# Last stage of a graph network kernel: second exponential and row turn exchanged on ScalarE, first slot sum and scan projection on TensorE

## What is computed

```python
# graph attention of the last layer
e = leaky_relu(s_src[src] + s_tgt[tgt], 0.2)
exp_e = exp(e - max(e)); denom = segment_sum(exp_e, tgt)
agg = segment_sum(proj[src] * (exp_e / (denom[tgt] + 1e-16))[:, :, None], tgt)
# scan (mamba) over x[perm]
xc, z = split(xs @ in_proj_w.T)
xc = silu(conv4(xc) + conv_b)
dbc = xc @ x_proj_w.T                          # 16 for dt, 16 for B, 16 for C
dt = softplus(dbc[:, :16] @ dt_proj_w.T + dt_proj_b)
dA = exp(dt[:, :, None] * A); dBx = (dt * xc)[:, :, None] * B[:, None, :]
h = dA_t * h + dBx_t;  y_t = h @ C_t           # for t in order, 16 states per channel
y = (y + xc * D_param) * silu(z);  return y @ out_proj_w.T
```

## Time and profile before

| | |
|---|---|
| median of 3 runs | 8897.0 us (8894.1 to 8900.4) |
| profiled execution | 8896.2 us, its span 8894.4 us |
| last stage | 6,424 us to 8,420 us of the span |
| PE busy in the span | 4623.8 us (52%) |
| DVE busy | 4836.3 us (54%) |
| ACT busy | 1231.8 us (14%) |
| POOL busy | 5163.8 us (58%) |

### The profile page before, as it was taken

How to read it: one execution, slowest core, us unless ns; L and a number is a source line. 1 busy time by engine, 2 the same in 40 slices (tenths; PEclk the granted TensorE clock), 3 DMA queues, 4 the chain that set the end, 5 groups by cost and what they waited for, 6 DMA issues and landing times. The chain is left out here.

```text
span 8894.4 us, 95573 instructions
## 1 busy us (share of the span) xinstructions
PE 4623.8 (52%) x18992; PEld 3629.7 (41%) x18993; DVE 4836.3 (54%) x11590; ACT 1231.8 (14%) x2744; POOL 5163.8 (58%) x4985
## 2 busy tenths in 40 slices
PE   4008244544457777656666555545454555554354
PEld 3002133333356666644444344433344444444333
DVE  9462388888822222245455344444466666666644
ACT  1002011111101111100000000001122222222111
POOL 0021366766667777677777677777655556555400
PEclk6557677677778888877777677777677777667676
DMA  0201256555423333233333233333222332222200
GB/s 8 75 16 52 59 143 170 161 159 162 130 80 94 92 90 94 69 84 99 92 95 95 63 83 96 89 92 92 75 85 83 91 91 83 86 86 80 71 6 9
DMA packets 485777, 772.81 MB, mean 87 GB/s; under 512 B 296031, under 2 KB 316310, under 8 KB 481979
## 3 DMA queue, kind: packets, MB, share of 16 engines
q0 software_dynamic: 265504, 666.90, 27.1%
q10 hardware_dynamic: 19838, 70.21, 2.1%
q1 hardware_dynamic: 200345, 34.81, 2.1%
HBM read 822.37 MB, written 46.03 MB: 98 GB/s over the span
## 5 line engine op out<-in xcount | busy, mean ns | idle before, releaser
L794 POOL DMA_INDIRECT gat_rows<-scratch_gat,gat_index x1856 | 1857.4, 1001 | 576.3 <-issue 540.0
L1071 PE MATMUL gat_ps<-gat_work,k_ident 128*128 128x256 f32 x3712 | 1214.3, 500 | 933.2 <-DVE gat_work L865 817.6
L1645 POOL DMA_INDIRECT m_rows<-scratch_gat,m_index x928 | 1097.1, 1182 | 861.0 <-DVE m_work L1934 581.5
L1071 PEld LDWEIGHTS gat_ps<-gat_work,k_ident 128*128 128x128 f32 x3712 | 941.3, 260 | 1213.2 <-issue 900.4
L794 POOL DMA_INDIRECT conv_rows<-scratch_kv,conv_index x928 | 931.9, 1004 | 410.7 <-issue 267.6
L1071 PE MATMUL conv_ps<-conv_work,k_ident 128*128 128x256 f32 x1856 | 668.4, 538 | 851.2 <-DVE conv_work L865 779.5
L1211 POOL DMA_INDIRECT rel_rows<-scratch_x,rel_index x928 | 926.7, 999 | 286.5 <-issue 273.8
L1071 PEld LDWEIGHTS conv_ps<-conv_work,k_ident 128*128 128x128 f32 x1856 | 511.8, 283 | 1008.2 <-issue 821.2
L1698 PE MATMUL m_ps<-m_work,k_ident 128*128 128x256 f32 x1664 | 524.2, 487 | 359.2 <-DVE m_work L1934 359.2
L1443 PE MATMUL rel_ps<-rel_factor,rel_rows 128*128 128x128 f32 x3712 | 581.6, 330 | 214.6 <-DMA rel_rows<-scratch_x,rel_index 214.6
L1443 PEld LDWEIGHTS rel_ps<-rel_factor,rel_rows 128*128 128x128 f32 x3712 | 563.2, 244 | 226.8 <-DMA rel_rows<-scratch_x,rel_index 154.5
(11 more groups left out here) (453 smaller groups left out, 7840.3 us busy)
## 6 DMA issues: line engine op xcount, KB each, us to landing
m_bc<-scratch_bc ACTq DMA_DIRECT2D x25, 2048.0 KB, 8.6
gat_rows<-scratch_gat,gat_index POOLq DMA_INDIRECT x1856
conv_rows<-scratch_kv,conv_index POOLq DMA_INDIRECT x928
rel_rows<-scratch_x,rel_index POOLq DMA_INDIRECT x928
m_rows<-scratch_gat,m_index POOLq DMA_INDIRECT x928
scratch_runs<-e_runs_sb SPq DMA_DIRECT2D x1, 12890.6 KB
scratch_kv<-p_row ACTq DMA_DIRECT2D x25, 256.0 KB
gat_index<-scratch_slots SPq DMA_DIRECT2D x232, 4.0 KB, 1.8
```

Source lines behind the costliest of these rows:

```text
L794: pool.indirect_dma_start(out=rows[b][:, s, :], out_offset=None, in_=table, in_offset=bass.IndirectOffsetOnAxis(ap=index[b][:, s:s + 1], a ...
L1071: ins = pe.matmul(ps_sum[min(b, 1)], ident, work[b][:, s, :], start=s == 0, stop=s == S - 1)
L1645: pool.indirect_dma_start(out=rows[b][:, s, :], out_offset=None, in_=dr["gat3"], in_offset=bass.IndirectOffsetOnAxis(ap=index[b][:, s:s + ...
```

## The change

```diff
@@ TensorE, tile(t, has_front, ahead) @@
                 w = Visit(pe, kp, t)
-                sum_slots(w, 0, 0)
                 if has_front:
                     front(t + 1)
+                sum_slots(w, 0, 0)
                 sum_states(t)
@@ ScalarE, tile(t, has_front, ahead) @@
                     spread_bc(t + 1)
+                exp(w, 0, 1)
                 if ahead:
                     turn(t + 2)
-                exp(w, 0, 1)
-                if ahead:
                     gates(t + 2)
                 store(t)
```

## The result

The changed kernel takes 8664.4 us (median of 4 runs, 8663.9 to 8673.8) against 8896.0 us (median of 4 runs, the three shown above and one of 8895.1): 0.974 of the time before, 95% interval 0.973 to 0.975. That is 231.6 us less. The prediction was 8659 us, within 8620 to 8735. The profiled execution of the changed kernel is the longest of its four runs, 8673.8 us; it starts tile 0 of the last stage at 6429.3 us, 5.1 us later than the profile before (6424.2), though nothing was changed ahead of it.

A forecast was written before the change was run, and what follows sets the result against it. VectorE's chain was taken to set the last stage's period, in five-chunk tiles together with GpSimd's gathers. 136 us (ScalarE's exchange) + 102 (TensorE's) = 238 us off 8896.2 is 8658, given as 8659 us; range 8620 to 8735.

The forecast's parts named there:

- The wait of the second chunk: VectorE's wait for ScalarE's exponential of the second gather, in tiles 0 to 22: 6.41 us falls to 0.27 us.
- The new wait for the scan input: VectorE waits some 0.5 us per tile for TensorE's scan input; the convolution still starts 5.6 us earlier.
- The second slot sum: TensorE's sum of the second gather takes 3.62 us instead of 5.40, so it doesn't delay the output product.
- the rival of the lower clock: More TensorE groups fall to 1.2 GHz and the second slot sum takes 6.54 us: 8727 us; chance 0.15.
- The third exponential: ScalarE's exponential of the third chunk, behind the store of the scan's output: its 2.62 us wait stays.
- TensorE gains clock: Rival: the denser last stage is granted 2.4 GHz sooner: 8624 us at most, 8641 us for half; chance 0.10.
- The projection: At a tile's head, the copy's wait falls from 4.57 to 0.7 us in 24 tiles; the projection takes 0.64 us.
- The moved slot sum costs nothing: TensorE's first slot sum, now after the projection, ends at least 2.8 us before the next state sums: no cost.
- Five-chunk tiles: Tiles 3 to 12: earlier release of the second gather's buffer shortens the next tile's gather wait, 0.7 us each, 7 us.
- part 1: ScalarE's exponential of the second chunk ahead of the turn of t + 2: 136 us in sum.
- the slower rival: GpSimd's gather issues, stretched under VectorE's scans, become the bound; slower only above 22.5 us per tile: 9000 us; chance 0.03.
- The signs of being wrong: Scan-input wait over 1.5 us, late output product, decays or first slot sum waited for, gather waits above 79.5 us.

The follow-up runs named there:

- the repeat: The changed kernel run once more, unchanged, as base for later kernels: 8665.4 us, 0.974 of the kernel before; its profiled run took 8662.5 us.
- a padded kernel: Three memsets of 1.85 us on GpSimd ahead of its wait for buffer 1, twice per tile, added to the changed kernel: 8810.3 us.
- the same eight extra matmuls: Eight matmuls that nobody reads, at the head of each tile ahead of the projection, added to the changed kernel: 8664.4 us.

## Why the prediction was right

- **The wait of the second chunk**: 150.6 us, forecast to fall to 0.27 us in each of 23 tiles. It fell to 6.2 us. Tile 23 had shown it before the change.
- **The new wait for the scan input**: forecast 0.5 us per tile, 11.5 in all; measured 21.4 in 22 tiles. The step that sized it took the pace of one tile's second sums of states (5.72 us) for all, though they already ranged from 5.2 to 6.8 us; they take 6.06 us on average in this profile, 6.45 in tile 11. It varies between runs: in the repeat's profile they take 5.87 us and the wait is 15.0 us in 20 tiles. That the convolution starts some 5.6 us earlier whatever the pace was right: E + 14.28 before, E + 9.35 here, with the sums 0.73 us longer.
- **The second slot sum**: I took 3.62 us by the neighbourhood of the earlier trace rows against the 5.40 of the earlier trace rows. It is 3.62 us in all 23 tiles, and the output product waits for y and not the other way. This is the choice between the forecast and the rival of the lower clock, and it was right for this group, with ScalarE's exchange alone as well.
- **The third exponential**: forecast to stay as it is. Its wait fell from 71.8 to 61.4 us over 23 tiles: 12 of them had waited 3.6 us behind an output product that took 2.07 us, and it takes 1.13 us now. The rival "TensorE gains clock" had named this. These 10 us are as much as the scan input cost too much.
- **The projection**: forecast 0.7 us of wait left in each of 24 tiles, with 0.9 as the upper bound; measured 1.07. The step that failed is "the projection takes 0.64 us": that row was read directly behind a slot sum, at a granted clock of 1.00, and the exchange puts a pause of 4 us or more there, behind which it is 0.50. With 1.08 us the term is 92.7 us instead of 101.6. The bound of 0.9 was too tight.
- **The moved slot sum costs nothing**: nearly. Its result is waited for by nobody, but TensorE's exchange alone brought 83 us where the projection's wait fell by 93; the difference appears as longer waits for exponentials. In the changed kernel these don't grow; there the wait for the scan input is the longer one, 21.4 and 15.0 us in the two profiles against 9.8 without the moved slot sum, where the second sums of states take 5.60 us on average.
- **Five-chunk tiles**: forecast 0.7 us more than the others in each, so 6.3 us of part 1. They gained 10.0 us each, the four-chunk tiles 9.7; of this the projection's wait gave 3.4 and 4.2, which leaves 6.7 and 5.5 us for part 1. The mechanism (gathers hold the next tile's first logits) was right: the release moved by 6.7 us on average, from E + 10.8 to E + 4.2, and the distance from it to the next tile's first logits stayed. In tile 11 it was 7455.51 - 7421.78 = 33.7 us before and is 7345.03 - 7311.23 = 33.8 now:

```profile
7345.03 0.19 DVE L1918 TENSOR_TENSOR m_logit<-m_rows,m_own 128x32 f32<-128x32 f32 x1 [0.55 <-DMA m_rows<-scratch_gat,m_index]
```

  So in these tiles neither the new wait for the scan input nor the shorter third one counts. What the forecast had in mind, a shorter wait for the gather itself, did not happen: at the first logits behind the ten tiles it went from 11.8 to 15.1 us (18.6 in the repeat), as VectorE comes there sooner.
- **GpSimd**: forecast 6 us left of its pause ahead of the release. 6.75 us is left in each of the tiles 1 to 22, and a padded kernel gives 5.3 us of room. The stretch of the issues grew by about 5 us per tile (6.4 to 11.4 in tile 12) and not by 6.4: beside the second scan only two of them are long, 1.98 and 4.64 us. That is under the 12.5 us from which the slower rival would have decided the tile.
- **The sum**: 238 us forecast, 231.6 measured. Of the 228.5 us in the stage the projection gave 92.7, where 102 were forecast; 135.8 are left for part 1, forecast at 136 (139.5 in the repeat). That part 1 came out so near is partly luck: the scan input cost 10 us more and the third exponential 10 us less than forecast.
- **The signs of being wrong**: two of those named came up, if barely. The wait for the scan input was over 1.5 us in two of 22 tiles (1.63 and 1.64), and the waits for gathers grew from 79.5 to 85.6 us. They didn't mean what they were to mean, as VectorE's earlier arrival at a gather shows as a longer wait without making the tile longer.

The rival of the lower clock holds for the projection, and not for the slot sum on which it rested. The rival of more clock holds for the output product. The sums of states moved both ways: on average the first of a tile takes 5.14 us instead of 6.02, the second 6.06 instead of 5.86.

## What to carry to other kernels

Where an in-order queue serves two chains, look for an operation that stands behind one whose input comes later than its own, and look in the same trace for an iteration without that neighbour (the last tiles of a pipeline): it shows the time that the exchange will give. A duration read directly behind other matmuls needs an upper bound of up to twice its size if the exchange puts it behind a pause: here 0.64 us became 1.08, and the output product takes 1.13 or 2.07. Before moving more work off a chain, ask tile by tile which engine holds the tile: a microsecond saved behind the point at which a gather chain starts came back as a wait for gathers in the five-chunk tiles, one saved ahead of it was kept.

## What was unexpected of the hardware

- A projection of two matmuls (48 columns of weights) takes 0.63 or 0.64 us at a granted clock of 1.00 and 1.08 us at 0.50, and the pause ahead of it does not decide which: behind the same eight extra matmuls (1.95 us) the clock was at 0.50 after a pause of 2.85 us and in another tile at 0.89 after one of 3.97 us.
- GpSimd's issue of an indirect DMA, 1.00 us otherwise, takes 4.64 us beside the second scan as beside the first.
- The same program took 8,896 or 8,897 us on two chips and 10,515 us on a third, with waits of up to 23 us for which the profile finds no releasing instruction, and with VectorE's busy time unchanged.
